# Value products of two key tiles in one visit, and a batch's sums read behind the next batch's second clip

## The chip, the cores and the metric

One core of one Trainium2 chip. The metric is the device time in microseconds (us) of one launch of the kernel. Engines are named as in the profile: PE is TensorE (its matmuls; PEld its weight loads), DVE VectorE, ACT ScalarE, POOL GpSimd, SP SyncE.

## The reference

A gated cross-attention block with a quantised feed-forward part, on 32 batches of 100 rows of 256, each with a context of 1444 rows of 256 (16 heads of 16), in float32. Cut to what matters:

```
q, k, v = proj(layernorm(x), Wq, bq), proj(ctx, Wk, bk), proj(ctx, Wv, bv)    # 16 heads
scores  = where(mask, q k^T / 4, -1e4), clipped to [-50, 50]
probs   = softmax(scores); probs = probs / (probs.sum(-1) + 1e-8)
delta   = layernorm(rs * ((probs @ v) @ Wo.T + bo)) * gamma + beta
x       = x + tanh(g_xattn) * delta
h       = silu(bitlinear(layernorm(x), w1)) * bitlinear(layernorm(x), w2)     
out     = x + tanh(g_ffn) * bitlinear(h, w3)
```

## The kernel before, in words

The 1444 keys of a batch are cut into 12 tiles (NT) of 121 (the last 113). Each engine runs a program of its own, written out by hand and ordered by semaphores: a loop over batches (`Fori`, two batches to an iteration, batches 3 to 30; 0, 1, 2 and 31 stand outside it), and in a batch 12 steps n = 0 to 11, one for a tile. What follows is the order within a step.

- TensorE (`batch`, L1287): first half of the scores of tile n (`scores`, 4 matmuls with 96 rows, split into high and low parts); first half of an item of the context projection of the next batch (`ctx_item`, L1223: key item `k_item`, 3 matmuls at L1204, or value item `v_item`, 6 matmuls at L1218; four items to a third of the context, two of each); the value products of tile n-2 (`pv`, L1168, LAG = 2: 32 matmuls at L1183 into the accumulator `pvb`, in four column groups of 32, each covering values and, by columns of ones in v_sb, the softmax sums); second half of the scores; second half of the item. At n = 0 and 1 the value products are of tiles 10 and 11 of the batch before. Between them stand small steps of the batches before and after: `h_turn` (n = 1) and `down` (n = 2) of two batches ago, `delta` (3), `x_turn` (4), `x_query` (5), `x2_turn` (6), `up` (7 to 10).
- ScalarE (`batch`, L608): exponential of each half tile (`exps`, L532, into one of 4 buffers e_sb), and between the two halves the copies of the context items (`k_head` L544, `v_out` L553), of h (`h_turned`, n = 2), the query (n = 6), the gate and up parts (n = 8 to 11).
- VectorE (`batch`, L946): `split_head` and `split_rest` (n = 1, 5, 9, L723 and L729), `k_rest` (L753, gives k_lo, on which the value items and the stacking DMAs wait), `clip` of tile n (L762, both halves at once, needs both exponentials), `attention_read` of the batch before (L817, reads `pvb` into oT and zt by 4 operations, at n = 1 ahead of the clip), `sums_inverse` (L829, shuffle and reciprocal, n = 1 behind clip and split_rest), `attention_out` (2), the two layer norms up to `x2_quant` (3 to 5), the hidden part (9 to 11).
- SyncE issues the loads and stacks the keys into k_st by DMA; GpSimd stacks the queries and does a few tiny steps.

The waits that touch the change: `pv` of a tile waits for its clip, for even tiles for v_done, and for tile 0 for z1 of the batch before (the sums are read before the accumulator is begun again). `scores` wait for the exponential two halves back. The exponential of tile n waits for the value products of tile n-4; `v_out` for those of the same tiles of the batch before. In the texts, "scores n.k" is half k (0 or 1) of tile n, and an "even" and an "odd" batch are the second and the first of a loop iteration.

Of the kernel before, what the change touches and what calls it, by code (L numbers as in the profile page):

```python
# [41 lines left out]
def flamingo_block(nc, x, ctxT, maskT, g_xattn, g_ffn, wqT, bq, wkT, bk, wvT, bv, woT, bo,  # L42
# [45 lines left out]
    LAG = 2  # L88
# [15 lines left out]
    with es:  # L104
# [552 lines left out]
        def _(dve):  # L657
# [288 lines left out]
            def batch(b, nxt, prev, prev2):  # L946
# [3 lines left out]
                for n in range(NT):  # L950
# [10 lines left out]
                        if n == 7:  # L961
                            q_rest(c)
                    if prev:
                        if n == 1:
                            attention_read(d)
                        if n == 2:
                            attention_out(d)
                        if n == 9:
                            hidden_gate(d, 0)
                        if n == 11:  # L970
                            hidden_gate(d, 1)
# [14 lines left out]
                        x_norm(c)  # L986
                    if prev:
                        if n == 1:
                            sums_inverse(d)
                        if n == 3:  # L990
                            delta_out(d)
                            delta_stats(d)
                            delta_aggr(d)
                            delta_gamma(d)
                        if n == 4:
                            first_sum(d)
                            x1_stats(d)
                            x1_aggr(d)
                        if n == 5:
                            x1_norm(d)  # L1000
                            x2_max(d)
                            x2_scale(d)
                            x2_round(d)
                            x2_quant(d)
                        if n == 10:
                            hidden_up(d, 0)
                        if n == 11:
                            hidden_up(d, 1)
                            h_max(d)
                            h_scale(d)  # L1010
                            h_round(d)
                            h_quant(d)
# [121 lines left out]
        def _(pe):  # L1134
# [152 lines left out]
            def batch(b, own, nxt, prev, prev2):  # L1287
                c, d = b.plus(1), b.plus(-1)
                first = not prev
                for n in range(NT):  # L1290
                    pb, pn = (b, n - LAG) if n >= LAG else (d, n - LAG + NT)
                    has_pv = n >= LAG or prev

                    def context(half):

# [2 lines left out]
                        if n < ITEM and own:  # L1298
                            ctx_item(b, n - ITEM + NT, half)

                    def attend(half):
                        if has_pv:
                            pv(pb, pn, half, first)

                    scores(b, n, 0)
                    context(0)
                    attend(0)
                    attend(1)
                    if prev2 and n == 1:
                        h_turn(b.plus(-2))  # L1310
                    if prev2 and n == 2:
# [106 lines left out]
```

## Time and profile before

| | before |
|---|---|
| time, median of 3 runs | 1603.58 us (1602.43 to 1604.38) |
| the profiled execution | 1603.54 us, span 1601.5 us |
| mean granted TensorE clock | 0.948 of full speed |
| PE busy | 1473.5 us (92%) |
| PEld busy | 1238.3 us (77%) |
| DVE busy | 1150.2 us (72%) |
| ACT busy | 996.0 us (62%) |
| POOL busy | 457.4 us (29%) |
| value products, L1183, PE | 356.4 us busy, 12288 matmuls |

The busy table says how long each engine had an instruction under way. The chain of section 4 of the page is followed back from the last instruction to whatever released each step, so it shows where the end is set, which busy shares don't. A row of the timeline gives start, duration, engine, line and operation, output from inputs with shapes, the count of instructions merged into it, and in square brackets how long the engine had been idle and what released it.

### The profile page before, as it was taken

To read this page: it belongs to the slowest core of one execution; us is meant where nothing else is said; L and a number is where in the kernel's file an instruction comes from. 1 tells how busy PE (TensorE), PEld (TensorE's weight loads), DVE (VectorE), ACT (ScalarE), POOL (GpSimd) and SP (SyncE) were. 2 spreads that over 40 slices of the span, in tenths; PEclk is the share of its full clock that TensorE was granted. 3 is DMA by queue.
4 is the path that set the end of the run, shared out by engine and by line. 5 is a ranking of instruction groups with operands and counts; after the bars stand their busy time and mean duration, and the time that the engine had idled before them with its cause. 6 is when DMAs were issued, how large, how long until landed. Compare 5 with 4: busy or idle time off the path is not lost.

```text
span 1601.5 us, 53405 instructions
## 1 busy us (share of the span) xinstructions
PE 1473.5 (92%) x19984; PEld 1238.3 (77%) x19984; DVE 1150.2 (72%) x2241; ACT 996.0 (62%) x1634; POOL 457.4 (29%) x759
## 2 busy tenths in 40 slices
PE   5699999999999999998999989999999999999982
PEld 4588887887878878787887878878787887878871
DVE  6567777686767777677677767768676777767764
ACT  2366766665667656676665766656575665666761
POOL 4322233222323313233321323312233331323310
PEclk9699999999999999999999999999999999999985
DMA  7366665555655556566565656556556564656520
GB/s 212 83 167 150 147 164 144 140 141 141 146 143 146 142 129 147 142 147 159 130 149 127 155 134 156 143 124 153 143 146 156 125 160 114 164 124 165 121 63 7
DMA packets 142458, 222.20 MB, mean 139 GB/s; under 512 B 29162, under 2 KB 135598, under 8 KB 142254
## 3 DMA queue, kind: packets, MB, share of 16 engines
q1 hardware_dynamic: 129966, 199.31, 51.9%
q0 software_dynamic: 12288, 19.69, 5.0%
q8 instruction: 187, 3.06, 0.9%
q14 instruction: 17, 0.14, 0.0%
HBM read 54.00 MB, written 3.28 MB: 36 GB/s over the span
## 4 chain that ended last, share of the span: by engine, by line
PE 55%; DVE 21%; issue 15%; ACT 4%; POOL 2%; DVEq 1%; DMA 0%; SPq 0%; ACTq 0%; POOLq 0%
PE sc L1163 16%; PE pvb L1183 13%; PE cb L1218 11%; PE cb L1204 9%; DVE c_lo L729 4%; ACT e_sb L532 3%; DVE k_lo L753 3%; PE mb L1269 3%; PE mb L1251 2%; DVE e_sb L762 1%; DVE x L868 1%; DVE tiny L914 1%; DVE dstat L872 1%; DVE tiny L885 1%; DVE dn L895 1%
## 5 line engine op out<-in xcount | busy, mean ns | idle before, releaser
L532 ACT ACTIVATE e_sb<-sc 121x800 f32<-121x800 f32 (+1 forms) x768 | 645.2, 841 | 526.9 <-PE sc L1163 526.6
L762 DVE TENSOR_SCALAR e_sb<-e_sb,hi_b 121x1600 f32<-121x1600 f32 (+1 forms) x384 | 411.3, 1071 | 330.4 <-ACT e_sb L532 330.3
L1163 PE MATMUL sc<-q_st,k_st 96*121 96x200 f32 (+1 forms) x3072 | 523.5, 294 | 51.6 <-issue 45.5
L1163 PEld LDWEIGHTS sc<-q_st,k_st 96*121 96x121 f32 (+1 forms) x3072 | 411.1, 191 | 121.7 <-issue 105.1
L1183 PE MATMUL pvb<-e_sb,v_sb 121*32 121x100 f32 x12288 | 356.4, 258 | 1.2 <-DVE e_sb L762 1.2
L1183 PEld LDWEIGHTS pvb<-e_sb,v_sb 121*32 121x32 f32 x12288 | 268.8, 112 | 94.4 <-issue 43.3
L1218 PE MATMUL cb<-wv_hi,c_hi 128*121 128x256 f32 (+1 forms) x768 | 227.6, 296 | 21.4 <-DVE k_lo L753 20.1
L1218 PE MATMUL cb<-wv_hi,c_lo 128*121 128x256 f32 (+1 forms) x768 | 216.5, 282 | 0.0
L1218 PE MATMUL cb<-wv_lo,c_hi 128*121 128x256 f32 (+1 forms) x768 | 216.0, 281 | 0.0
L418 POOL TENSOR_SCALAR x_ve<-mv 100x1 f32<-100x1 f32 x32 | 7.3, 227 | 677.8 <-DVE mv L778 677.8
L462 POOL DMA_DIRECT2D q_st<-bd_hi x256 | 142.7, 561 | 118.1 <-DVE bd_lo L808 114.2
L753 DVE SCALAR_TENSOR_TENSOR k_lo<-cb,bk_c,k_hi 128x484 fp32r<-128x484 f32 (+1 forms) x192 | 134.5, 701 | 48.8 <-ACT k_hi L544 48.7
L1218 PEld LDWEIGHTS cb<-wv_hi,c_hi 128*121 128x121 f32 (+1 forms) x768 | 142.1, 185 | 30.6 <-DVE k_lo L753 27.4
L1204 PE MATMUL cb<-c_hi,wk_hi 128*128 128x484 f32 (+1 forms) x384 | 160.3, 417 | 0.0
L1204 PE MATMUL cb<-c_lo,wk_hi 128*128 128x484 f32 (+1 forms) x384 | 151.2, 394 | 0.0
L1204 PE MATMUL cb<-c_hi,wk_lo 128*128 128x484 f32 (+1 forms) x384 | 149.7, 390 | 0.0
L1218 PEld LDWEIGHTS cb<-wv_hi,c_lo 128*121 128x121 f32 (+1 forms) x768 | 141.4, 184 | 0.1
L1218 PEld LDWEIGHTS cb<-wv_lo,c_hi 128*121 128x121 f32 (+1 forms) x768 | 140.6, 183 | 0.0
L544 ACT ACTIVATE k_hi<-cb,bk_c 128x484 fp32r<-128x484 f32 (+1 forms) x192 | 127.8, 666 | 4.6 <-PE cb L1204 4.6
L729 DVE TENSOR_TENSOR c_lo<-c_in,c_hi 128x968 fp32r<-128x968 f32 (+1 forms) x96 | 112.1, 1168 | 0.0
L553 ACT ACTIVATE v_sb<-cb 121x512 f32<-121x512 f32 x160 | 96.0, 600 | 20.7 <-PE cb L1218 20.7
L462 POOL DMA_DIRECT2D q_st<-bd_lo x128 | 104.9, 820 | 0.1
(139 smaller groups left out, 1593.2 us busy)
## 6 DMA issues: line engine op xcount, KB each, us to landing
k_st<-k_hi SPq DMA_DIRECT2D x512, 121.0 KB, 3.0
c_in<-in_ctxT SPq DMA_DIRECT2D x64, 484.0 KB, 3.6
k_st<-k_lo SPq DMA_DIRECT2D x256, 121.0 KB, 3.1
k_st<-k_hi SPq DMA_DIRECT2D x256, 119.0 KB
c_in<-in_ctxT SPq DMA_DIRECT2D x32, 476.0 KB, 3.5
k_st<-k_lo SPq DMA_DIRECT2D x128, 119.0 KB
q_st<-bd_hi POOLq DMA_DIRECT2D x256, 50.0 KB, 3.2
q_st<-bd_lo POOLq DMA_DIRECT2D x128, 50.0 KB, 3.4
```

Of the source, the lines that this page charges most:

```text
L462: nc.gpsimd.dma_start(q_st[b.par][QR * part:QR * (part + 1), :, j, :].bitcast(f32), src[QR * j:QR * (j + 1), :, :, :].rearrange("p k a s - ...
L532: nc.scalar.activation(e_sb[n % NE][0:TL[n], k * SW:(k + 1) * SW].rearrange("p (o c) -> p o c", o=2), sc[q % NSC][0:TL[n], :, 0:2 * PW], A ...
L544: nc.scalar.activation(k_hi[slot][:, o, 0:CL[u]], cb[o][:, 0:CL[u]], ACT.Identity, bias=bk_c[:, o:o + 1]).then_inc(k_hi_done, 1)
L553: nc.scalar.activation(v_sb[0:TL[n], n:n + 2, :, 0:4:3, :].rearrange("p n q a d -> p (n q) a d"), cb[i][0:TL[n], :].rearrange("p (q a d) - ...
L729: V.tensor_tensor(c_lo[slot][:, :, 0:w], c_in[slot][:, :, 0:w], c_hi[slot][:, :, 0:w].bitcast(f32), ALU.subtract).then_inc(split_done, 1)
L753: V.scalar_tensor_tensor(k_lo[slot][:, o, 0:w], cb[o][:, 0:w], bk_c[:, o:o + 1], k_hi[slot][:, o, 0:w].bitcast(f32), ALU.add, ALU.subtract ...
L762: V.tensor_scalar(e, e, E_LO, hi_b[b.par][0:TL[n], n:n + 1], ALU.max, ALU.min).then_inc(clip_done, 1)
L1163: last = T_.matmul(sc[q % NSC][0:TL[n], e // 2, (e % 2) * PW:(e % 2 + 1) * PW], k_st[n // TPC][:, pr // NQ, pr % NQ, t0:t0 + TL[n]], q_st[ ...
L1183: last = T_.matmul(pvb[QR * j:QR * (j + 1), col:col + S], v_sb[0:TL[n], n, pr, 2 * a:2 * a + 2, :].rearrange("p x d -> p (x d)"), e[0:TL[n ...
L1204: last = T_.matmul(cb[o][:, 0:w], wt[:, k, o * P:(o + 1) * P], ct[slot][:, k, 0:w], start=i == 0, stop=i == 5)
L1218: last = T_.matmul(cb[i][0:TL[n], half * H:(half + 1) * H], ct[slot][:, k, t0:t0 + TL[n]], wt[:, k, :], start=(k == 0 and a == 0), stop=(k ...
L1269: last = T_.matmul(mb[0:S, 0:FH], x2T[:, k, :], w12q[:, k, c0:c0 + FH], start=k == 0, stop=k == KT - 1)
```

## The change

At even tiles TensorE makes no value products; at an odd tile n it makes those of tiles n-3 and n-2, one behind the other, both halves of each (at n = 1 tiles 10 and 11 of the batch before). On VectorE `attention_read` of the batch before moves from ahead of clip 1 to behind clip 1 and `split_rest`, directly ahead of `sums_inverse`.

```diff
@@ VectorE, batch
                     if prev:
-                        if n == 1:
-                            attention_read(d)
                         if n == 2:
                             attention_out(d)
...
                     if prev:
                         if n == 1:
+                            attention_read(d)
                             sums_inverse(d)
@@ TensorE, batch
                 for n in range(NT):
-                    pb, pn = (b, n - LAG) if n >= LAG else (d, n - LAG + NT)
-                    has_pv = n >= LAG or prev
+                    pair = [(b, i) if i >= 0 else (d, i + NT) for i in (n - LAG - 1, n - LAG)]
+                    has_pv = n % 2 == 1 and (n >= LAG + 1 or prev)
...
-                    def attend(half):
+                    def attend():
+
                         if has_pv:
-                            pv(pb, pn, half, first)
+                            for pb, pn in pair:
+                                pv(pb, pn, 0, first)
+                                pv(pb, pn, 1, first)
 
                     scores(b, n, 0)
                     context(0)
-                    attend(0)
-                    attend(1)
+                    attend()
```

## Rows read from the trace of the kernel before

**Rows 1.** The page: busy time, the chain by engine, the value products' group.
```profile
PE 1473.5 (92%) x19984; PEld 1238.3 (77%) x19984; DVE 1150.2 (72%) x2241; ACT 996.0 (62%) x1634; POOL 457.4 (29%) x759
...
PE 55%; DVE 21%; issue 15%; ACT 4%; POOL 2%; DVEq 1%; DMA 0%; SPq 0%; ACTq 0%; POOLq 0%
...
L1183 PE MATMUL pvb<-e_sb,v_sb 121*32 121x100 f32 x12288 | 356.4, 258 | 1.2 <-DVE e_sb L762 1.2
```

**Rows 2.** Waits of the whole span: engine, line, awaited; us, times, longest.
```profile
PEld cb L1218 <- DVE k_lo L753: 27.4, 34, 9.7
PEld mb L1257 <- DVE x2q L899: 22.4, 30, 8.0
PE sc L1163 <- issue: 45.5, 13, 4.1
```

**Rows 3.** Timeline of PE: scores with and without value products ahead of them.
```profile
812.29 0.38 PE L1204 MATMUL cb<-c_hi,wk_lo 128*128 128x476 f32 x1
...
812.92 0.29 PE L1218 MATMUL cb<-wv_hi,c_hi 128*121 128x256 f32 x1
...
826.05 0.38 PE L1204 MATMUL cb<-c_hi,wk_lo 128*128 128x484 f32 x1
826.37 0.90 PE L1183 MATMUL pvb<-e_sb,v_sb 121*32 121x100 f32 x32
827.20 0.67 PE L1163 MATMUL sc<-q_st,k_st 96*121 96x200 f32 x4
827.70 0.40 PE L1204 MATMUL cb<-c_hi,wk_hi 128*128 128x484 f32 x1
```

**Rows 4.** Timeline of ACT, DVE and PE, tiles 1 to 3 of an even batch.
```profile
812.04 0.84 ACT L532 ACTIVATE e_sb<-sc 121x800 f32<-121x800 f32 x1 [1.12 <-PE sc L1163]
812.20 0.42 DVE L823 TENSOR_SCALAR oT<-pvb,submask 128x200 f32<-128x200 f32 x1
813.54 1.04 DVE L762 TENSOR_SCALAR e_sb<-e_sb,hi_b 121x1600 f32<-121x1600 f32 x1
817.99 0.38 PE L1218 MATMUL cb<-wv_hi,c_hi 128*121 128x256 f32 x1 [0.57 <-DVE k_lo L753]
```

**Rows 5.** Timeline of PE, ACT and DVE, tiles 0 to 3 of an odd batch.
```profile
758.78 1.13 PE L1163 MATMUL sc<-q_st,k_st 96*121 96x200 f32 x4 [3.82 <-issue]
767.54 0.84 ACT L532 ACTIVATE e_sb<-sc 121x800 f32<-121x800 f32 x1 [1.12 <-PE sc L1163]
768.57 1.04 DVE L762 TENSOR_SCALAR e_sb<-e_sb,hi_b 121x1600 f32<-121x1600 f32 x1
773.01 0.39 PE L1218 MATMUL cb<-wv_hi,c_hi 128*121 128x256 f32 x1
```

**Rows 6.** Timeline of ACT, DVE and PE, tiles 5 and 6 of the even batch.
```profile
827.90 0.84 ACT L532 ACTIVATE e_sb<-sc 121x800 f32<-121x800 f32 x1 [0.49 <-PE sc L1163]
828.87 1.05 DVE L762 TENSOR_SCALAR e_sb<-e_sb,hi_b 121x1600 f32<-121x1600 f32 x1
832.93 0.26 PE L1257 MATMUL mb<-identb,x2q 100*128 100x100 bf16 x2 [0.20 <-DVE x2q L899]
```

**Rows 7.** Timeline of PE, ACT and DVE, tiles 10 and 11 of the even batch.
```profile
843.68 0.70 PE L1163 MATMUL sc<-q_st,k_st 96*121 96x200 f32 x4
844.42 0.84 ACT L532 ACTIVATE e_sb<-sc 121x800 f32<-121x800 f32 x1 [0.54 <-PE sc L1163]
847.40 0.08 DVE L753 DVE_READ_ACCUMULATOR k_lo<-cb,bk_c,k_hi  x1
847.78 0.29 PE L1218 MATMUL cb<-wv_hi,c_hi 128*121 128x256 f32 x1
```

**Rows 8.** Timeline of PE: the wait at tile 3 of an early batch.
```profile
110.32 0.38 PE L1218 MATMUL cb<-wv_hi,c_hi 128*121 128x256 f32 x1 [1.42 <-DVE k_lo L753]
```

**Rows 9.** Windows: length; PE, PEld, DVE, ACT, POOL busy; granted clock, DMA share, GB/s.
```profile
854.20:901.00 46.80, 46.49 (x623) 39.12 (x624) 31.80 (x64) 30.46 (x51) 14.40 (x23) 0.94 0.56 134
...
1562.00:1564.00 2.00, 0.07 (x2) 0.07 (x3) 1.85 (x6) 0.00 (x0) 0.00 (x0) 0.65 0.03 8
```

## The prediction, made before the change was run

> **What bounds the kernel now.** I read the page's busy table and chain first [rows 1], then the waits of TensorE's weight loads [rows 2], then single batches in the timeline. TensorE is busy 92% of the span, which looks as if all of it were TensorE's time. The chain says otherwise: it spends 55% on TensorE, 21% on VectorE, 4% on ScalarE. Three places in each batch (numbering tiles 0 to 11 within a batch, "scores n.k" the k-th half of tile n) carry it off TensorE:
> - Gate 1, the value item of the context at tile 3: it waits for k_lo from VectorE, whose queue of tiles 1 and 2 ends just then (idle 0.57 us in the even batch [rows 4], and TensorE goes straight into it at 773.01 in the odd one [rows 5]; 34 weight-load waits of this kind in the run [rows 2]).
> - Gate 2, the transposes x2_turn at tile 6: they wait for x2q from VectorE, 30 times in the run [rows 2], 0.20 us in the batch that I follow [rows 6].
> - Gate 3, the value item at tile 11: no wait now, but k_lo is ready at 847.48 and the matmul starts at 847.78, so its slack is 0.3 us [rows 7].
> Between gates TensorE is the bound. So I ask of each of its savings on which side of a gate it falls.
>
> **What a visit costs.** With value products between a key item and the scores, from the item's last matmul to the first one after the scores is 827.70 - 826.05 = 1.65 us; without, 812.92 - 812.29 = 0.63 us [rows 3]. The visit costs 1.02 us. Its 32 matmuls take 0.90 us from first start to last end [rows 3], and one of them 0.258 us in the mean [rows 1], so 31 steps are 0.64 us and 32 are 0.66 to 0.67; I go on with 0.67. The other 0.35 us is going in and out. A second tile in the same visit costs 0.67 us, and a visit removed gives 0.35. The second tile is not in the trace; its bounds are 0.67 (seamless) and 0.83 (start of the products to start of the scores, 827.20 - 826.37 [rows 3]). I take 0.67, because the two halves of a tile already join without a gap inside that 0.90.
> The trace shows this 0.35 us around the products and does not say why. The Trainium skill, TensorEngine Tiling (Array Packing), Key Properties, says that changing the tiling mode drains the engine; by that rule alone, with TensorE the bound throughout, the time would fall. That is the first rival below; the gates are why I don't forecast it.
>
> **The change part by part.** Visits: batch 0 has 10 and becomes 5, the 31 others go from 12 to 6, so 191 are removed (the two tiles at the end already stand together). Waits added on TensorE: none; both tiles' clips are two tiles old or more. e_sb and v_sb come free up to a tile later, but always ahead of the scores that follow in TensorE's own queue, so I put that at nothing; if this cover were gone, ScalarE's exponentials would wait a visit, 1.5 us. The sums z1 are read a step later, and their user on TensorE (tile 0's value products) moves from tile 2 to tile 3, so that wait costs nothing. No DMA is moved on a queue: stack_k of the last third starts with k_lo, about 1 us later, but is needed only at tile 8.
> Now a batch, segment by segment, in the even batch of the rows:
> - a. Gate 1 to clip 5. Now value tiles 1, 2, 3 in three visits, then tiles 0 to 3 in two: +0.67 - 0.35 = +0.32 to scores 5.1. Exponential 5.1 ends at 828.74 and clip 5 starts at 828.87 [rows 6], so 0.13 of it is slack. +0.19 us.
> - b. Clip 5 to gate 2, 4.06 us [rows 6]: VectorE's queue, nothing in it changes. The products of tile 4 that leave tile 6 leave a place where TensorE was to wait anyway: gain 0.
> - c. Gate 2 to gate 3. To scores 10.0 now 843.68 - 832.93 = 10.75 us with tiles 5, 6, 7 in three visits, then 4 to 7 in two: 11.07. From there TensorE alone needed 4.10 us (843.68 to 847.78) and without tile 8's visit would need 3.08. But exponential 10.0 starts 0.74 behind these scores and k_lo is done 3.06 behind it [rows 7]; with 0.06 from there to the matmul (my choice; a tenth more or less would move the total by 3 us), 3.86. Sum 14.93 against 14.85: +0.08 us. Nearly the whole visit is lost to a new wait of 0.8 us.
> - d. Gate 3 to scores 11.1: tiles 8 and 9 in place of 9: +0.67, and +0.09 because the first weights behind a wait are not loaded ahead (the matmul behind the wait at gate 1 takes 0.38 us [rows 4], one without a wait 0.29 [rows 3]). +0.76 us.
> - e. Scores 11.1 to the next gate 1. This is where the moved read of the sums counts. VectorE runs without a pause from clip 11 to gate 1, and attention_read (813.54 - 812.20 = 1.34 us) fills the time in which clip 1 could not start, as exponential 1.1 ends only at 812.88 [rows 4]. Behind the change clip 1 stands first and waits for it. One visit fewer ahead brings that end to 812.53, so clip 1 starts at 812.57, 0.97 earlier; the sums' 1.34 us then stand behind it, and the shuffle that needs z1 comes right behind z1 with no work between (not in the trace; between 0 and the 0.42 us of one such operation [rows 4]; I take 0.15, nearer the lower end, since only the end of z1 is uncovered, not all of it). 1.34 - 0.97 + 0.15 = +0.52 us. TensorE's savings at tiles 0, 1 and 2 are all inside this stretch and bring nothing; at tile 2 `down` would wait for ScalarE's hT instead.
> - e in the odd batches, behind the loop's end, where TensorE waits 3.82 us for nothing that the profile shows and VectorE catches up: exponential 1.1 runs 767.54 to 768.38, clip 1 starts at 768.57 [rows 5]. It could start at 768.07, only 0.50 earlier: 1.34 - 0.50 + 0.15 = +0.99 us.
> Sum: even batch 0.19 + 0.08 + 0.76 + 0.52 = +1.55 us, odd with 0.99 for the 0.52 +2.02 us. The loop's end is seen 13 times [rows 2]; 30 batches (1 to 30) have the full pattern: 13 x 2.02 + 17 x 1.55 = +52.6 us. Batch 0 has no earlier batch's work on VectorE: up to 5 x 0.35 = -1.7. The last batch has no context items and ends on its own chain: 0. Total +51 us. The profiled execution took 1603.54 us (span 1601.5), the median is 1603.58: 1654 us.
>
> **The rivals.**
> - Faster: TensorE is the bound at the gates too, and 191 x 0.35 = 67 us fall off: 1537 us. For it: busy 92%, and waits of only 0.57 and 0.20 us at the gates, so that VectorE need be only a little early. Against: it decides only if VectorE and ScalarE reach each gate over 0.35 us sooner than they do now, and the change puts 1.34 us of VectorE's work behind a wait instead. Partial forms lie between 1537 and 1600. Chance 0.12.
> - No change: segment e costs nothing more (the DVE queue absorbs it), and a, c, d are cancelled by parts of visits saved. 1604. Chance 0.06.
> - Slower, but by the sums alone: the gates 2 and 3 don't bite and a to d cancel, e stays: 13 x 0.99 + 17 x 0.52 = +22 us: 1625. Chance 0.17.
> - My sum, with sizes off by a third either way: 1635 to 1672. Chance 0.50.
> - The visit isn't one: the second tile begins with a gap of its own, so each double visit costs 0.83 instead of 0.67 for it. Of the six in a batch, those at tiles 3, 5, 7, 9, 11 are on the path: 31 x 5 x 0.16 = +25 us: 1679. Chance 0.07.
> - TensorE's clock falls in the longer waits. A wait of 1.42 us at gate 1 in an early batch was followed by a matmul of 0.38 us, as at full speed [rows 8]; a stretch of 2 us near the end in which TensorE was busy for 0.07 has a mean granted clock of 0.65, so it went from 2.4 to 1.2 GHz within it. I expect a wait at tile 2 and one of over 1 us at tile 3, close together, which lies between the two. What a fall costs: the odd batch, which begins behind the loop's end at 1.2 GHz, has a mean clock of 0.94 over 46.8 us [rows 9], so it loses 2.8 us; in 17 even batches 48 us: 1702. Chance 0.08.
>
> **How the numbers follow.** Likeliest: 1654 us. Left out at the bottom are the faster cases (0.12) and some of no change; at the top the clock in part. Range 1608 to 1690. 0.2% is 3.2 us, about what a measurement can tell from no change: faster 0.12, same 0.06, slower 0.82.
>
> **What would show it.** Right: the products' groups of 64 matmuls take about 1.55 us; at gate 1 TensorE waits over 1 us instead of 0.57, with clip 1 starting right behind exponential 1.1; waits of about 1.2 us at x2_turn (0.20 and a visit) and 0.8 us at the value item of tile 11; VectorE's wait for e_sb rises. TensorE's busy time falls by some 60 us while the span grows. Wrong: the value item of tile 3 goes without a wait, or the middle of the span shows two batches shorter than now.

## The result, and the profile after

The changed kernel takes 1707.09 us in the median (1704.86 to 1709.60, four runs) against 1603.98 us for the kernel before in the same series: ratio 1.0645, 95% interval 1.0626 to 1.0663. It is slower by 103 us. The prediction had the sign and most of the mechanism, but said 1654 and no more than 1690: half of the loss was missing from it. The profiled execution took 1709.6 us with a mean granted clock of 0.936 of full speed, where the profiled one of before took 1603.54 us at 0.948.

The page of the changed kernel: the span, the busy table, the granted clock in 40 slices, and the group of the value products (busy time, mean ns of one, idle time ahead of it).

```profile
span 1707.6 us, 53405 instructions
...
PE 1455.9 (85%) x19984; PEld 1268.7 (74%) x19984; DVE 1174.8 (69%) x2241; ACT 980.4 (57%) x1634; POOL 432.4 (25%) x759
...
PEclk9799999998999989899998999999998998999995
...
L1182 PE MATMUL pvb<-e_sb,v_sb 121*32 121x100 f32 x12288 | 322.9, 260 | 1.2 <-DVE e_sb L762 1.2
```

Against [rows 1], the same 19984 matmuls keep TensorE busy for 18 us less, and the span is 106 us longer: the savings are there and the waits outgrew them. The value products fell from 356.4 to 322.9 us. The slices at 8 in the middle of the clock's row are new.

The waits of the changed kernel (us in total, times, longest):

```profile
PEld cb L1217 <- DVE k_lo L753: 88.7, 65, 9.4
PEld mb L1256 <- DVE x2q L899: 54.9, 30, 8.0
PEld mb L1268 <- ACT gs L601: 19.1, 45, 1.6
DVE x L868 <- POOL d_r L438: 15.9, 30, 1.1
```

The waits for k_lo were 34 in [rows 2] and are 65: all three gates now wait in each batch. Two more had no place in the sum: `up` waits for ScalarE's gs 45 times (3 times before), and VectorE waits for GpSimd's d_r 30 times (once before).

The timeline of TensorE in the changed kernel: an odd batch from the loop's end (806.96) through gate 1 (822.44), gate 2 (839.36) and gate 3 (854.68), then gates 1 and 2 of the even batch behind it (871.26, 886.68). Columns as in [rows 3].

```profile
806.96 1.13 PE L1162 MATMUL sc<-q_st,k_st 96*121 96x200 f32 x4 [3.80 <-issue]
...
822.44 0.57 PE L1217 MATMUL cb<-wv_hi,c_hi 128*121 128x256 f32 x1 [1.56 <-DVE k_lo L753]
...
824.00 2.42 PE L1182 MATMUL pvb<-e_sb,v_sb 121*32 121x100 f32 x64
826.35 0.67 PE L1162 MATMUL sc<-q_st,k_st 96*121 96x200 f32 x4
...
831.98 1.59 PE L1182 MATMUL pvb<-e_sb,v_sb 121*32 121x100 f32 x64
...
839.36 0.26 PE L1256 MATMUL mb<-identb,x2q 100*128 100x100 bf16 x2 [1.37 <-DVE x2q L899]
...
843.84 0.70 PE L1162 MATMUL sc<-q_st,k_st 96*121 96x200 f32 x4
...
846.55 0.70 PE L1162 MATMUL sc<-q_st,k_st 96*121 96x200 f32 x4
...
850.75 0.69 PE L1162 MATMUL sc<-q_st,k_st 96*121 96x200 f32 x4
...
854.68 0.38 PE L1217 MATMUL cb<-wv_hi,c_hi 128*121 128x256 f32 x1 [0.54 <-DVE k_lo L753]
...
857.08 0.64 PE L1162 MATMUL sc<-q_st,k_st 96*113 96x200 f32 x4
...
866.98 0.99 PE L1283 MATMUL mb<-w3q,hT 128*100 128x256 bf16 x6 [0.89 <-ACT hT L594]
...
871.26 0.38 PE L1217 MATMUL cb<-wv_hi,c_hi 128*121 128x256 f32 x1 [1.55 <-DVE k_lo L753]
...
873.68 0.67 PE L1162 MATMUL sc<-q_st,k_st 96*121 96x200 f32 x4
...
886.68 0.26 PE L1256 MATMUL mb<-identb,x2q 100*128 100x100 bf16 x2 [1.33 <-DVE x2q L899]
```

The same places of the kernel before, in the stretch ahead of [rows 6] (gate 2 at 787.88, scores 8.0, 9.0 and 10.0, gate 3 at 802.82, scores 11.1):

```profile
787.88 0.26 PE L1257 MATMUL mb<-identb,x2q 100*128 100x100 bf16 x2 [0.15 <-DVE x2q L899]
...
791.74 0.69 PE L1163 MATMUL sc<-q_st,k_st 96*121 96x200 f32 x4
...
795.23 0.69 PE L1163 MATMUL sc<-q_st,k_st 96*121 96x200 f32 x4
...
798.72 0.70 PE L1163 MATMUL sc<-q_st,k_st 96*121 96x200 f32 x4
...
802.82 0.30 PE L1218 MATMUL cb<-wv_hi,c_hi 128*121 128x256 f32 x1
...
804.46 0.65 PE L1163 MATMUL sc<-q_st,k_st 96*113 96x200 f32 x4
```

These two, with [rows 4] to [rows 6], give the bookkeeping between gates, in us. The even batch runs from one gate 2 to the next: 832.93 - 787.88 = 45.05 before, 886.68 - 839.36 = 47.32 after.

| segment | before | after | change | forecast |
|---|---|---|---|---|
| c, gate 2 to gate 3 | 14.94 | 15.32 | +0.38 | +0.08 |
| d, gate 3 to scores 11.1 | 1.64 | 2.40 | +0.76 | +0.76 |
| e, scores 11.1 to gate 1, even | 13.53 | 14.18 | +0.65 | +0.52 |
| e, loop's end to gate 1, odd | 14.23 | 15.48 | +1.25 | +0.99 |
| a and b, gate 1 to gate 2, even | 14.94 | 15.42 | +0.48 | +0.19 |
| even batch | 45.05 | 47.32 | +2.27 | +1.55 |

In the odd batch gate 1 to gate 2 takes 839.36 - 822.44 = 16.92 us, 1.50 more than in the even one. The first scores behind gate 1 start 826.35 - 822.44 = 3.91 us later there, and 873.68 - 871.26 = 2.42 us later in the even batch, so the 1.5 us all lie there. It is the clock. The windows of the changed kernel (length; PE, PEld, DVE, ACT, POOL busy; granted clock, DMA share, GB/s), the even batch's and then the odd one's:

```profile
872.00:876.00 4.00, 4.00 (x83) 3.52 (x83) 2.10 (x5) 0.84 (x1) 0.94 (x3) 1.00 0.76 166
...
822.00:826.00 4.00, 3.56 (x61) 3.33 (x64) 2.54 (x7) 0.23 (x1) 0.94 (x3) 0.57 0.51 116
```

Behind a wait of 1.56 us the granted clock is 0.57, that is mostly 1.2 GHz instead of 2.4, and 64 value products take 2.42 us instead of 1.59. Behind the next gate 1, with a wait of 1.55 us, it stays at 1.00. From the batch with gate 1 at 207.91 to the one at 1586.96 there are 29 waits of 1.54 to 1.57 us at gate 1; the clock falls behind 14 of them, and behind two longer ones in the early batches (3.62 and 1.98 us): 16 x 1.5 = 24 us. It isn't the odd batch as such, nor the loop's end ahead of it. From gate 1 at 310.44 to the one at 924.78 it is the odd batch each time; behind 1012.34, where the loop comes round again, it is the even one four times running. The first of these:

```profile
1075.02 0.57 PE L1217 MATMUL cb<-wv_hi,c_hi 128*121 128x256 f32 x1 [1.56 <-DVE k_lo L753]
```

Now 17 even batches of 2.27, 13 odd ones of 0.38 + 0.76 + 1.25 + 0.48 = 2.87, and the clock: 38.6 + 37.3 + 24 = 100 us, with the 1.7 us that batch 0 was to win 98, of the 106 between the two profiled executions. Of the 8 that are left, 5.4 are in TensorE's waits at the loop's end: 50.9 us in total, 13 times, against 45.5 before [rows 2].

### The profile page after: what moved, and what is told of

The parts are those of the page before. It is cut to its first block, busy times and chain, and to the rows that moved or that the text cites. A ratio compares the mean times of both kernels' runs of the same rounds, so it can differ in the third digit from the quotient of the medians.

```text
span 1707.6 us, 53405 instructions
## 1 busy us (share of the span) xinstructions
PE 1455.9 (85%) x19984; PEld 1268.7 (74%) x19984; DVE 1174.8 (69%) x2241; ACT 980.4 (57%) x1634; POOL 432.4 (25%) x759
## 4 chain that ended last, share of the span: by engine, by line
PE 53%; DVE 19%; issue 15%; ACT 6%; POOL 5%; DVEq 1%; DMA 0%; SPq 0%; POOLq 0%; ACTq 0%
PE pvb L1182 15%; PE sc L1162 13%; PE cb L1203 10%; PE cb L1217 9%; DVE c_lo L729 4%; ACT e_sb L532 3%; PE mb L1268 2%; POOL d_rstd L436 2%; DVE k_lo L753 2%; PE mb L1250 2%; ACT k_hi L544 1%; DVE e_sb L762 1%; PE mb L1276 1%; DVE x L868 1%; DVE tiny L885 1%
## 5 line engine op out<-in xcount | busy, mean ns | idle before, releaser
L1162 PE MATMUL sc<-q_st,k_st 96*121 96x200 f32 (+1 forms) x3072 | 510.6, 290 | 58.1 <-issue 50.9
L1162 PEld LDWEIGHTS sc<-q_st,k_st 96*121 96x121 f32 (+1 forms) x3072 | 424.3, 192 | 110.5 <-issue 84.0
L1182 PE MATMUL pvb<-e_sb,v_sb 121*32 121x100 f32 x12288 | 322.9, 260 | 1.2 <-DVE e_sb L762 1.2
L1182 PEld LDWEIGHTS pvb<-e_sb,v_sb 121*32 121x32 f32 x12288 | 279.6, 114 | 48.1 <-issue 35.0
L1217 PE MATMUL cb<-wv_hi,c_hi 128*121 128x256 f32 (+1 forms) x768 | 235.7, 307 | 77.2 <-DVE k_lo L753 77.1
L1217 PE MATMUL cb<-wv_hi,c_lo 128*121 128x256 f32 (+1 forms) x768 | 221.2, 288 | 0.0
L462 POOL DMA_DIRECT2D q_st<-bd_hi x256 | 170.4, 669 | 118.1 <-DVE bd_lo L808 112.1
L1217 PEld LDWEIGHTS cb<-wv_lo,c_hi 128*121 128x121 f32 (+1 forms) x768 | 145.3, 189 | 0.0
L1203 PEld LDWEIGHTS cb<-c_hi,wk_lo 128*128 128x128 f32 x384 | 76.2, 198 | 12.7
```

The costliest lines, as they stand in the source:

```text
L462: nc.gpsimd.dma_start(q_st[b.par][QR * part:QR * (part + 1), :, j, :].bitcast(f32), src[QR * j:QR * (j + 1), :, :, :].rearrange("p k a s - ...
L1162: last = T_.matmul(sc[q % NSC][0:TL[n], e // 2, (e % 2) * PW:(e % 2 + 1) * PW], k_st[n // TPC][:, pr // NQ, pr % NQ, t0:t0 + TL[n]], q_st[ ...
L1182: last = T_.matmul(pvb[QR * j:QR * (j + 1), col:col + S], v_sb[0:TL[n], n, pr, 2 * a:2 * a + 2, :].rearrange("p x d -> p (x d)"), e[0:TL[n ...
L1203: last = T_.matmul(cb[o][:, 0:w], wt[:, k, o * P:(o + 1) * P], ct[slot][:, k, 0:w], start=i == 0, stop=i == 5)
L1217: last = T_.matmul(cb[i][0:TL[n], half * H:(half + 1) * H], ct[slot][:, k, t0:t0 + TL[n]], wt[:, k, :], start=(k == 0 and a == 0), stop=(k ...
```

## The experiments

All times are medians; a ratio is to the kernel before in runs on the same chip, with its 95% interval. A difference between two experiments of different chips is taken over these ratios or the medians, since the kernel before kept within 1602 to 1604 us on all of them.

### The two parts apart

**Pairs alone.** The changed kernel with the read of the sums put back:

```diff
                     if prev:
+                        if n == 1:
+                            attention_read(d)
                         if n == 2:
                             attention_out(d)
...
                         if n == 1:
-                            attention_read(d)
                             sums_inverse(d)
```

> The changed kernel with the read of the sums put back ahead of the second clip, so only the double visits are left. Theory G (gates: what counts is how late VectorE and ScalarE reach three waits of TensorE): the stretch from the transposes of h to the value item of tile 3 loses what the read added, 0.62 us in the even and 1.25 us in the odd batch (0.97 and 1.46 measured between the two traces, plus the visit of 0.35 saved in front, less 0.55 in the odd one that the earlier keys give back), some 29 us in all; the wait there falls below 1 us, so the clock no longer falls in it and another 24 us go. About 1654 us, with x2_turn still waiting about 1.3 us and the value item of tile 11 about 0.5. Rival V (the double visit itself starves the other engines, and the place of the read is of no account): within 10 us of the changed kernel, 1700 or more.

Measured: 1657.66 us (1655.69 to 1661.77), ratio 1.0352 [1.0333, 1.0371]. The timeline of TensorE in this kernel, gates 1 and 2:

```profile
840.79 0.38 PE L1218 MATMUL cb<-wv_hi,c_hi 128*121 128x256 f32 x1 [0.90 <-DVE k_lo L753]
856.21 0.26 PE L1257 MATMUL mb<-identb,x2q 100*128 100x100 bf16 x2 [1.35 <-DVE x2q L899]
...
858.16 2.74 PE L1183 MATMUL pvb<-e_sb,v_sb 121*32 121x100 f32 x64
```

From gate 1 to gate 2 it is 856.21 - 840.79 = 15.42 us, as in the changed kernel, and the even batch takes 46.66 us: exactly c, d, a and b of the table (0.38 + 0.76 + 0.48 = 1.62). The wait at gate 1 is 0.90 us in place of 1.55, and the clock falls behind none of these. But it falls behind gate 2: in six batches the wait of 1.33 to 1.35 us there is followed by 1.2 GHz (2.74 us for 64 products above), while the changed kernel, with the same waits, shows no such fall in the same part of the run. So the pairs cost 55 us, some 9 of them by the clock, and the read of the sums, in their presence, 49 more.

**The read alone.** The kernel before with `attention_read(d)` moved:

```diff
                     if prev:
-                        if n == 1:
-                            attention_read(d)
...
                         if n == 1:
+                            attention_read(d)
                             sums_inverse(d)
```

> The kernel before with only the read of the sums moved behind the second clip, single visits kept. Theory G: worse than pairing with it, because tile 0's value products at tile 2 now wait for the sums: they started at 813.73 in the even batch and the sums would be read at about 816.4, so the value item of tile 3 comes 1.9 us later (even) and 2.4 us later (odd): +63 us, 1667 us, and up to 1700 where the wait of 2.7 us lets the clock fall. Rival V: the move of the read alone is worth at most 10 us, 1604 to 1614.

Measured: 1770.32 us (1760.23 to 1775.01), ratio 1.1025 [1.0986, 1.1065], with a mean granted clock of 0.885. A miss on the high side. Its wait for zt, and its timeline of TensorE at tile 2:

```profile
PE pvb L1182 <- DVE zt L826: 80.6, 31, 2.7
...
849.35 1.56 PE L1182 MATMUL pvb<-e_sb,v_sb 121*32 121x100 f32 x32 [2.63 <-DVE zt L826]
```

Alone, the read stalls tile 0's value products at tile 2 by 2.6 us in each of 31 batches (the prediction rested on these products being at tile 3 when paired), and the clock falls behind it: these 32 products take 1.56 us instead of 0.90. Each part is slower alone, and moving the read without pairing is the worst of all.

### Is it the clock?

**Work put into the wait.** The changed kernel, with the first half of the scores of tile 3 made three times over, so that TensorE does 8 more matmuls just ahead of gate 1:

```diff
-                for e in range(SPB):
+                for e in [*range(SPB)] * (3 if n == 3 and k == 0 else 1):
```

> The changed kernel in which TensorE makes the first half of the scores of tile 3 three times over (same results, written into the same place before ScalarE is told), which puts 8 more matmuls per batch, some 0.8 to 1.3 us of work, into the wait of 1.55 us at the value item of tile 3. Theory C (in every other batch this wait lets the clock fall, at 1.5 us a time): the added work is free and the clock stays, 1707 - 24 = 1683 us, matmuls of 0.28 us behind the wait in all batches. Rival (the clock falls there for another reason, such as the end of the loop before it): 1707 or more, and every other batch still has matmuls of 0.41 us behind the wait.

Measured: 1688.37 us (1684.93 to 1696.31), ratio 1.0551 [1.0519, 1.0583]: 19 us less than the changed kernel, with 256 matmuls more. Its timeline of TensorE:

```profile
849.02 0.99 PE L1283 MATMUL mb<-w3q,hT 128*100 128x256 bf16 x6 [0.89 <-ACT hT L594]
...
853.30 0.38 PE L1217 MATMUL cb<-wv_hi,c_hi 128*121 128x256 f32 x1 [0.70 <-DVE k_lo L753]
```

and gate 2 of the batch before it:

```profile
819.80 0.26 PE L1256 MATMUL mb<-identb,x2q 100*128 100x100 bf16 x2 [1.36 <-DVE x2q L899]
...
821.34 2.85 PE L1182 MATMUL pvb<-e_sb,v_sb 121*32 121x100 f32 x64
```

The wait shrinks to 0.70 us, and the gate opens no earlier: from `down` to the value item it is 853.30 - 849.02 = 4.28 us, as in the changed kernel (871.26 - 866.98). Behind gate 1 the clock now falls in none of the 29 batches, where it fell in 14, and gate 1 to gate 2 takes 15.35 us in the mean of them instead of 16.08: 21 us less. That the wait lets the clock fall at gate 1, and that filling it prevents this, is shown. This is the part of the loss that the prediction gave a chance of 0.08.

The 19 us of the whole run are not that number alone. The falls moved on in part: behind gate 2, where the wait is 1.32 to 1.38 us as in the changed kernel, eight batches now show one (some 12 us). And TensorE's waits at the loop's end add up to 40.1 us instead of 50.9, for no reason that the profile shows. That the total came out near the 24 expected is in part luck.

### The chain from the sums to gate 2

**k_lo ahead of the sums.** If gate 1 is late because the read stands ahead of `k_rest`, swapping them should free it:

```diff
-                    if own and n in (ITEM - 3, ITEM - 2):
-                        k_rest(b, NCH - 1, n - (ITEM - 3))
+                    if own and n == ITEM - 3:
+                        k_rest(b, NCH - 1, 0)
...
                         if n == 1:
+                            if own:
+                                k_rest(b, NCH - 1, 1)
                             attention_read(d)
```

> The changed kernel with VectorE's k_rest of tile 2 put ahead of the read of the sums, so that the value item of tile 3 needs nothing that stands behind it. Theory G: the wait of 1.55 us at tile 3 goes, and the fall of the clock with it (24 us); TensorE then comes about 1.5 us earlier to the next gate, x2_turn, where VectorE's queue has only some 2 us of idle time to give, so about half to two thirds of the 1.5 us stay: 1707 - 24 - 30 x 0.9 = 1656 us. Rival V: the double visits set the time, only the clock's part goes, 1683 us.

Measured: 1707.10 us (1702.02 to 1708.53), ratio 1.0655 [1.0637, 1.0673]: no gain at all, a plain miss by 51 us. The wait at gate 1 is gone. Its timeline of TensorE at gate 2, and of VectorE ahead of it:

```profile
878.99 0.26 PE L1258 MATMUL mb<-identb,x2q 100*128 100x100 bf16 x2 [1.81 <-DVE x2q L899]
881.37 2.15 PE L1184 MATMUL pvb<-e_sb,v_sb 121*32 121x100 f32 x64
...
868.14 0.41 DVE L782 TENSOR_SCALAR xn<-x_in,mv,x_rstd 100x256 f32<-100x256 f32 x1 [0.77 <-POOL x_rstd L420]
...
872.41 0.49 DVE L868 SCALAR_TENSOR_TENSOR x<-dn,d_r,x_res 100x256 f32<-100x256 f32 x1 [1.24 <-POOL d_r L438]
```

What was saved at gate 1 (1.7 us between scores 11.1 and gate 1) is paid between gate 1 and gate 2 (17.26 us instead of 15.42): VectorE now stands waiting for GpSimd's x_rstd and d_r, TensorE waits 1.81 us for x2q, and the clock falls behind gate 2 instead, in 16 batches (2.15 us for 64 products in this one). Gates 1 and 2 are not two queues but one chain through VectorE and GpSimd, which begins at the sums and ends at x2q.

**That wait taken out.** To show it, d_r is replaced by a constant (which leaves the delta's scale by rstd out of the result) and the second statistics get a tile of their own:

```diff
-                dve.wait_ge(pool_post, D_P.after(b, "r"))
...
-                dv(V.scalar_tensor_tensor(x1[:, :], dn, d_r[:, :], x_res[b.par][:, :], ALU.mult, ALU.add))
+                dv(V.scalar_tensor_tensor(x1[:, :], dn, minus_half[:, :], x_res[b.par][:, :], ALU.mult, ALU.add))
...
-                dv(V.bn_aggr(dmv[:, :], dstat[:, :]))
+                dv(V.bn_aggr(dmv2[:, :], dstat[:, :]))
```

On the changed kernel:

> The changed kernel in which the sum x + delta on VectorE takes a constant in place of the factor r that GpSimd works out (so delta isn't normalised by its variance; GpSimd still computes r, and x1's statistics go to a tile of their own). It removes the wait of 0.51 us for r behind clip 4. Theory G: the queue to x2_turn moves up only until clip 5 meets exponential 5.1, which ends 0.24 us ahead of it now: 30 x 0.24 = -7 us, 1700 us, with the wait at x2_turn going from 1.35 to about 1.1. Rival (GpSimd's wait is on the path with all of its length): -15 us, 1692.

Measured: 1705.74 us (1702.66 to 1708.36), ratio 1.0641 [1.0620, 1.0661]. Gate 1 to gate 2 shrinks from 15.42 to 885.52 - 870.30 = 15.22 us in this kernel's timeline:

```profile
870.30 0.38 PE L1217 MATMUL cb<-wv_hi,c_hi 128*121 128x256 f32 x1 [1.56 <-DVE k_lo L754]
885.52 0.26 PE L1256 MATMUL mb<-identb,x2q 100*128 100x100 bf16 x2 [1.15 <-DVE x2q L899]
```

The total moved by 1.4 us, less than these medians can tell apart. So the wait for d_r is 0.2 us of the 0.29 by which a and b missed, no more, as long as gate 1 is late.

The same together with k_lo ahead of the sums:

> The same constant in place of r, in the kernel with k_rest of tile 2 put first (1707 us, where x2_turn waits 1.81 us and VectorE waits 1.24 us for r). Theory G (what tile 3 gave back was lost again in the chain of VectorE and GpSimd to x2q): VectorE's 1.24 us go, x2_turn waits about 0.6 us, the clock no longer falls behind it: 30 x 1.2 + 15 x 1.5 = -58 us, about 1650. Rival (something else holds x2q): within 10 us of 1707.

Measured: 1649.23 us (1647.05 to 1651.71), ratio 1.0290 [1.0272, 1.0308]. Now the 51 us that the previous swap was to bring are there (58 below it), and the clock doesn't fall behind either gate. Neither edit moves the total alone; both together give 58 us, as was forecast for one serial chain through both gates (36 us of the chain and 22 of the clock; the 16 falls that are gone make 24).

### Which pairs cost, and which pay

In the next kernels the value products follow a table by step (this is the kernel before, and the entries are the distances of the tiles made in that step):

```diff
-                    pb, pn = (b, n - LAG) if n >= LAG else (d, n - LAG + NT)
-                    has_pv = n >= LAG or prev
+                    lag = {4: (), 5: (3, 2), 8: (), 9: (3, 2)}.get(n, (2,))
+                    tiles = [(b, n - i) if n >= i else (d, n - i + NT) for i in lag if n >= i or prev]
...
-                            pv(pb, pn, half, first)
+                        for pb, pn in tiles:
+                            pv(pb, pn, 0, first)
+                            pv(pb, pn, 1, first)
```

**Two pairs**, 2/3 and 6/7: the second tile of each falls in a stretch in which TensorE has slack to gain, and none stands right behind a gate.

> The kernel before with only two double visits: tiles 2 and 3 at tile 5, tiles 6 and 7 at tile 9 (tiles 4 and 8 without value products); all others, and the sums, as before. By theory G these are the two pairs whose removed visit lies where TensorE is the bound (tiles 4 and 8), while the other pairs remove one beside a wait (tiles 0, 2, 6, 10). Each gives up to 0.35 us, less a small wait for ScalarE's gate copy at tile 8: 31 x (0.3 + 0.25) = -17 us, 1586 us, faster than before. Rival V (any double visit costs): slower than 1603, about a third of the changed kernel's loss without the sums: 1620.

Measured: 1598.81 us (1594.95 to 1601.90), ratio 0.9973 [0.9963, 0.9982]. The even batch takes 44.68 us (45.05 before), 0.37 less where 0.55 was expected. Faster, but by 4 us instead of 17.

**Three pairs**, with tiles 10/11 of the batch before as well (`0: (), 1: (3, 2)` added):

> As the kernel with two double visits, and tiles 10 and 11 of the batch before in one visit at tile 1 too. Theory G: nothing in the even batch, where VectorE sets the time of tile 3, and 0.34 us in the odd one (restart of the loop to the value item of tile 3 took 13.89 in the kernel with pairs only, 14.23 in the kernel before): 14 x 0.34 = -5 us against two double visits, 1581 us. Rival V: about half of the loss of all pairs, 1630.

Measured: 1588.67 us (1586.11 to 1589.62), ratio 0.9907 [0.9890, 0.9924]: 14 to 15 us faster than the kernel before, and the fastest of the study. The even batch is again 44.68 us long, so this third pair pays in the odd batches: from the loop's end to gate 1 it is 13.97 us in their mean instead of 14.48. Against the kernel before, the 0.37 us of the even batch are worth 6 of the 14 us, in 17 batches; the others lie in the batches with the loop's end (49.88 us in the mean instead of 50.47).

**All pairs but 8/9**, on the pairs alone:

```diff
-                    pair = [(b, i) if i >= 0 else (d, i + NT) for i in (n - LAG - 1, n - LAG)]
-                    has_pv = n % 2 == 1 and (n >= LAG + 1 or prev)
+                    lag = {10: (2,), 11: (2,)}.get(n, (3, 2) if n % 2 == 1 else ())
+                    pair = [(b, n - i) if n >= i else (d, n - i + NT) for i in lag if n >= i or prev]
+                    has_pv = len(pair) > 0
```

> The kernel with pairs only (1658 us) in which the pair of tiles 8 and 9 is undone: tile 8 again at tile 10, tile 9 at tile 11. By the gates this pair moves the products of tile 8 from a place where TensorE waits anyway (the wait of about 0.5 us for k_lo at tile 11 takes what tile 10 saved) to one where it doesn't: undoing it should give back d, 0.76 us, less 0.17 in front of the gate: 31 x 0.6 = -18 us, about 1640, with the wait at tile 11 gone. If instead the loss is spread evenly over the five pairs that are left: (1658 - 1603 - what the sums' neighbour costs) / 5, some -10 us, 1648, and if every pair saves a visit of 0.35 that tile 10 can use, +11 us, 1669.

Measured: 1620.72 us (1619.62 to 1631.57), ratio 1.0129 [1.0098, 1.0161]: 37 us below the pairs alone. The even batch gains 0.57 us, as was expected (46.66 to 46.09); 17 of these are 10 us. The 13 odd ones give 7 more by the same 0.57, which makes 17 for the pair, near the 18 expected. The rest isn't the pair's own price: the waits at the loop's end fell from 49.4 to 41.7 us, and the clock fell behind gate 2 in three batches instead of six (4.5 us).

Then each of the three others was added alone to the three pairs. Pair 8/9:

> The kernel with three double visits (1588.7 us) and tiles 8 and 9 in one visit at tile 11 as a fourth. By the gates: tile 10 can use 0.24 us of the visit it loses, tile 11 gets 0.67 + 0.09: +0.5 us in each of 31 batches, +16 us, 1605. If the 37 us that undoing this pair gave in the other kernel were its own price, 1626, and most of it would lie at the loop's end, in the odd batch.

Pair 4/5:

> The same with tiles 4 and 5 in one visit at tile 7 as the fourth. The visit that goes from tile 6 stands ahead of x2_turn, which waits for VectorE anyway (0.33 us now, 1.3 then): nothing is saved, and tile 7 pays 0.67 us: 31 x 0.67 = +21 us, 1610. If a visit removed were worth its 0.35 wherever it stands, 31 x -0.35: 1578.

Pair 0/1:

> The same with tiles 0 and 1 in one visit at tile 3 as the fourth. The visit that goes from tile 2 stands ahead of down, which then waits for ScalarE's hT, and in the even batch ahead of the wait for k_lo: nothing is saved; tile 3 pays 0.67 us, and VectorE's clips 3 and 4 come as much later: 31 x 0.6 = +19 us, 1607. If a visit removed were worth its 0.35 wherever it stands: 1578.

Measured: 1605.28 us (1603.80 to 1606.98), ratio 1.0017 [1.0008, 1.0027] for 8/9; 1609.96 us (1605.59 to 1624.98), 1.0064 [1.0035, 1.0093] for 4/5; 1601.25 us (1595.46 to 1602.90), 0.9985 [0.9974, 0.9997] for 0/1. So +17, +21 and +13 us on the three pairs. Each is paid at its own gate. For 4/5 the 21 us are the least certain, with executions from 1605.59 to 1624.98 us: in the profiled one the clock fell behind gate 2 in ten batches (some 15 us), and the waits at the loop's end were 5 us shorter than in the three pairs. The waits of the three pairs, of those with 8/9, with 4/5 and with 0/1:

```profile
PEld cb L1218 <- DVE k_lo L753: 25.9, 20, 9.1
PEld mb L1257 <- DVE x2q L899: 26.7, 30, 8.0
```

```profile
PEld cb L1218 <- DVE k_lo L753: 47.4, 51, 9.0
```

```profile
PEld mb L1257 <- DVE x2q L899: 55.1, 30, 8.0
```

```profile
PE mb L1284 <- ACT hT L594: 28.0, 32, 0.9
```

With 8/9, gate 3 begins to wait (31 waits more, 21.5 us more). With 4/5, gate 2's wait grows by 0.95 us in each of 30 batches: nearly the 1.02 us of the visit that tile 6 no longer makes. With 0/1, `down` waits for hT in each batch where tile 2 makes no products. The scores that follow the double visit come later by a tile's 0.67 us, and with them the exponentials that the next gate hangs on.

### Can gate 1 be relieved in the fastest?

Three pairs with k_rest ahead of the shuffle:

> The kernel with three double visits (1588.7 us) with VectorE's k_rest of tile 2 put ahead of the shuffle and the reciprocal of the sums. In the even batch TensorE waits 0.76 us for it at tile 3 and k_hi is there 2.4 us earlier; VectorE has 0.96 us of idle time ahead of clip 3 to give, so the 0.76 can go through to clip 4: 15 x 0.6 = -9 us, 1580, if x2_turn follows. Rival (as with all pairs: what tile 3 gives is taken back at x2_turn, whose queue on VectorE has the same work in it): within 3 us of 1589.

Measured: 1603.08 us (1601.74 to 1605.70), ratio 1.0005 [0.9996, 1.0014]: the whole gain lost. Three pairs, and the kernel before, with `split_rest(c, 0)` moved from tile 1 to tile 3:

```diff
+                            split_rest(c, 0)
...
-                    if nxt and n % 4 == 1:
+                    if nxt and n in (5, 9):
```

> The kernel with three double visits (1588.7 us), in which VectorE's split_rest of the next batch's first third (1.08 us a time) moves from between clip 1 and the shuffle of the sums to behind x_aggr at tile 3, where VectorE has 0.25 and 0.96 us of idle time. Theory S (the length of the batch is the serial chain from the sums to x2q, so whatever stands ahead of the sums' steps on VectorE counts, and whatever stands in its idle time doesn't): both k_lo for tile 3 and oT come 1.08 us earlier, the wait of 0.76 us at tile 3 of the even batch goes, and x2_turn is reached 0.7 us earlier there: 15 x 0.7 = -10 us, 1578. Rival (GpSimd's answers for x_rstd and r, 0.77 and 1.24 us of waiting in the kernel with k_rest first, take it back as they did there): within 3 us of 1589.

> The kernel before with the same move of split_rest alone, all visits single. Theory S: the wait of 0.57 us at tile 3 in the even batch goes, x2_turn follows: 15 x 0.5 = -8 us, 1595. Rival: GpSimd's answers or exponential 3.1 hold VectorE, within 3 us of 1603.

Measured: 1598.57 us (1594.22 to 1601.48), ratio 0.9978 [0.9967, 0.9988] on the three pairs, 10 us above them; 1599.95 us (1598.46 to 1601.86), ratio 0.9990 [0.9981, 0.9999] on the kernel before. Both changes to the three pairs were expected to gain, and both lost. The waits of the first (k_rest ahead):

```profile
PEld mb L1259 <- DVE x2q L899: 39.5, 30, 8.0
DVE x L868 <- POOL d_r L438: 37.6, 31, 1.3
```

TensorE's wait for x2q rises from 26.7 to 39.5 us, and VectorE's for d_r from 15.6 to 37.6; with the late split on three pairs they are 39.4 and 37.3. It is the same as with k_lo ahead of the sums: what gate 1 gets, gate 2 hands back, where VectorE waits for GpSimd's answers. In the even batch it gives nothing (44.63 us for the late split, 44.68 without it) or costs (45.10 with k_rest ahead). In the 13 odd batches both lose, and the traces show where. With the late split, gate 1 comes 0.13 us earlier behind the loop's end in the mean, and gate 1 to gate 2 takes 15.52 us instead of 14.74: 13 x 0.65 = 8 us. With k_rest ahead it is 0.44 earlier and 0.77 more. So gate 2 hands back more there than gate 1 got; why gate 1 got so little isn't settled.

## Why the prediction was right or wrong

**The visit: right.** 64 products take 1.59 us (831.98) against 0.90 for 32 [rows 3], so the second tile costs 0.69 where 0.67 was taken. The rival in which each second tile begins with a gap of 0.16 is out.

**Which gates, and that they take the savings: right.** The waits came where they were said: 1.33 to 1.37 us at gate 2 (forecast 1.2), 1.55 at gate 1 (over 1), 0.54 at gate 3 (0.8). The first rival, TensorE as the bound throughout, is out: all savings in front of a gate turned into waits. But TensorE's busy time fell by 18 us and not by some 60; even with the pairs alone, and fewer falls of the clock, it fell by 36. The 0.35 us around a visit is only partly time that the trace counts as busy.

**Segment d: exact.** +0.76.

**Segment e: right in kind, a little small.** Clip 1 does start right behind exponential 1.1. The timeline of VectorE in the changed kernel:

```profile
865.20 1.05 DVE L762 TENSOR_SCALAR e_sb<-e_sb,hi_b 121x1600 f32<-121x1600 f32 x1 [0.29 <-ACT e_sb L532]
```

From scores 11.1 to clip 1 it is 8.12 us, 0.96 less than before (forecast 0.97), and the shuffle waits 0.15 for zt, as taken. From clip 1 to gate 1 it is 6.06 against 4.45 us, 1.61 more, where 1.34 + 0.15 = 1.49 was forecast. In the odd batch clip 1 came only 0.37 us earlier and not 0.50 (816.38 in this trace, 9.42 behind the loop's end, against 9.79 in [rows 5]). Together 17 x 0.13 + 13 x 0.26 = 5.6 us missing.

**Segment c: undersized; the term that failed is the way to scores 10.0.** Gate 3's new wait and the 3.93 us from scores 10.0 to it (forecast 3.86) were right. But the way to scores 10.0 grew by 0.55 and not by 0.32. Scores 8.0 to 9.0 took 3.49 us with a visit before, 2.47 without one; they take 846.55 - 843.84 = 2.71 now. There `up` waits for gs (45 waits in the waits view). I take this wait for the cause of the 0.24 us; no run took it away, so that isn't shown. The prediction's words were "Waits added on TensorE: none", by a look at the clips and buffers alone. The prediction gave every saved 1.02 us its full price and didn't ask what is next behind it at tiles 7 to 10. 30 x 0.30 = 9 us.

**Segments a and b: undersized.** The prediction said of b that nothing in VectorE's queue changes. In it stands a round trip to GpSimd. The timeline of VectorE and GpSimd in the changed kernel, then the times of GpSimd's step over the whole run (min/median/max in ns), in the kernel before and in the changed one:

```profile
878.53 1.06 DVE L762 TENSOR_SCALAR e_sb<-e_sb,hi_b 121x1600 f32<-121x1600 f32 x1 [0.24 <-ACT e_sb L532]
880.10 0.48 DVE L868 SCALAR_TENSOR_TENSOR x<-dn,d_r,x_res 100x256 f32<-100x256 f32 x1 [0.51 <-POOL d_r L438]
...
878.50 1.12 POOL L436 TENSOR_TENSOR d_rstd<-d_ve,minus_half 100x1 f32<-100x1 f32 x1
```

```profile
L436 POOL TENSOR_TENSOR d_rstd<-d_ve,minus_half x32: 547/547/640, 116.9 to 1575.6; 100x1 f32<-100x1 f32 x32
```

```profile
L436 POOL TENSOR_TENSOR d_rstd<-d_ve,minus_half x32: 547/1124/1364, 119.1 to 1681.7; 100x1 f32<-100x1 f32 x32
```

Once clip 4 runs beside it, GpSimd's power of a 100x1 column takes 1.12 us, where the median before was 0.55, and VectorE stands 0.51 us behind its own clip for the answer. The step goes with the clip in every batch: in the changed kernel the 29 that have a whole clip beside them take 1.11 to 1.36 us, the three with at most 0.21 us of one take 0.55 or 0.56. With k_lo ahead of the sums, which moves the clips, 31 have none beside them and take 0.55 or 0.56; the one that has, with another operation of VectorE next to it, takes 1.59. The Trainium skill, GPSIMD Engine Reference, Specifications, says that GpSimd's interfaces to SBUF are shared with VectorE and that the two contend when VectorE's operation is in a 2-port performance mode or has two inputs in SBUF. The rows agree as far as the clip slows the step; that the clip is one of these operations no run here shows. Taking out the wait gave back 0.20 of the 0.29 us missed. 30 x 0.29 = 9 us.

**The clock: the step that failed most.** Its chance was 0.08, on the ground that a wait of 1.42 us at gate 1 in an early batch left a matmul at full speed [rows 8], while the expected wait was put at "over 1 us". The sum held nothing for it. The actual wait of 1.55 us was followed by 1.2 GHz in 14 of 29 batches (16 falls in the run, 24 us), and with work put into the wait none was. One row at 1.42 us was read as a licence for all that lies near it. It was no bound: of 29 waits alike to within 0.03 us in this same kernel 15 were harmless, and at gate 2 waits of 1.32 to 1.37 us were harmless in the changed kernel and not in six batches of the pairs alone. The rival was also priced wrong in place and number: all even batches at 2.8 us (48 us) in place of 16 batches at 1.5.

**The sum of the misses.** 103 measured less 51 forecast is 52 us: the clock 24, a and c 18, e 6, the longer waits at the loop's end 5. That is 53, but the closeness is worth little: e in the odd batches is read from one batch, and the mean of the 13 is 1.08 us where the table has 1.25. The three good pairs are worth 14 us of gain and the three bad ones, each added alone, 13 + 21 + 17 = 51 us of loss; together they cost 69 (1588.67 to 1657.66), so 18 us appear only when all stand together. Of these the traces show 9 as falls of the clock behind gate 2 (six batches of the pairs alone, none of the three pairs in the same stretch) and 4 in the waits at the loop's end (49.4 against 45.1 us). Pair 8/9 has the same price both ways, 17 us, once these two are told apart. At the loop's end TensorE waits 2.6 to 4.4 us for nothing that the profile shows; in the kernels of this study the 13 waits add up to between 39.7 us (with 4/5) and 50.9 (the changed kernel). Behind it TensorE is at 1.2 GHz for a time that differs from iteration to iteration, 4.7 to 6.1 us in the kernel before and 3.6 to 9.7 with two pairs. What sets either isn't settled by these runs, and differences of 5 to 10 us between two kernels can come from there. The prediction took it as unchanged.

The band for sizes off by a third is 1637 to 1671 by the prediction's own sum, not 1635 to 1672; nothing hangs on it.

**The read of the sums.** Between the pairs alone and the whole change lie 49 us. The traces of the two (54 us apart) give 21 to the clock behind gate 1, less 9 for the falls behind gate 2 that go; and VectorE's queue costs more than the table says, since with the pairs alone gate 1 came earlier in the odd batches: 13.56 us behind the loop's end in the mean against 15.33, so 17 x 0.65 + 13 x 1.77 = 34 us, where 22 was forecast against the kernel before.

## What to carry to other kernels

A saving counts up to the next gate only, and behind each saving stands a next wait: ask which it is, for every stretch, also where nothing waits now. When the work of two gates runs through one engine pair in turn, relieving the first alone moves the wait to the second; look for the chain, not the place. Put pieces of work together only where the piece that becomes longer doesn't stand between a gate and what the next gate hangs on: three of the six pairs were worth 14 us, and the other three cost over 50.

When a change makes the bounding engine wait in the middle of its work, give the fall of its clock a real chance unless the trace shows many waits of that length without one. And look behind the next wait as well: filling the one at gate 1 moved some of the falls to gate 2.

## What the hardware showed that was not expected

- More work was faster: with 256 extra matmuls put into TensorE's wait at gate 1 no fall of the clock was left behind it, and the kernel took 19 us less.
- The same wait of 1.54 to 1.57 us at gate 1 is followed by 1.2 GHz in 14 of 29 batches and by 2.4 GHz in the others. Waits of 1.32 to 1.38 us at gate 2 are followed by 1.2 GHz in none of 28 batches of the changed kernel and in eight of the one with extra matmuls. Waits of 0.69 to 0.92 us at gate 1, with the pairs alone and with the extra matmuls, never are.
- GpSimd's power operation on 100x1 takes 0.55 us alone and 1.11 to 1.36 us beside a whole one of VectorE's clips of 121x1600, in all 29 batches of the changed kernel where they meet.
- The time at 1.2 GHz behind the loop's end differs between iterations of one kernel (3.6 to 9.7 us with two pairs) with nothing in the trace that tells why.
